# Softmax probabilities kept packed and multiplied with the values as 64-row tiles, in a gated cross-attention block on Trainium2

## The chip, the cores and the metric

The kernel runs on one core of a Trainium2 chip. The metric is the device time of one execution in microseconds; before the change it is 1895.37 us, the median of 3 runs (1894.49 to 1895.81).

## The reference

Everything is 32-bit float. There are 32 batches of 64 rows of width 512, 32 heads of width 128, 64 queries and 64 keys per batch and head. What is computed:

```python
x = x + tanh(g_xattn[0]) * xattn(layernorm(x), ctx, mask, bias, Wq, Wk, Wv, Wo)
x = x + tanh(g_ffn[0]) * ffn(layernorm(x), weight, bias, lora_A, lora_B, lora_start_indices)

def xattn(hq, hkv, mask, bias, Wq, Wk, Wv, Wo):
    q, k, v = (hq @ Wq), (hkv @ Wk), (hkv @ Wv)          # each reshaped to batch, 64, 32 heads, 128
    score = einsum('bqhd,bkhd->bhqk', q, k) / sqrt(128) + bias
    probs = softmax(where(mask, score, -inf))            # and 0 where masked
    return einsum('bhqk,bkhd->bqhd', probs, v).reshape(b, 64, 4096) @ Wo
```

`ffn` is a 512 by 512 layer with a bias and a low-rank addend per batch.

## The kernel before

**Precision.** Each operand of a product is split in two fp32r tiles, hi and lo (lo is what the rounding of hi left over). `mm3` (L172 to L176) makes a product of three matmuls (hi by hi, lo by hi, hi by lo). `both` (L192 to L197) makes it of two: the two parts of the left operand are loaded as weights in turn (L196 the hi part, L197 the lo part), and the hi and lo parts of the right one stream past side by side, so that a matmul is 256 columns wide. In the profile a matmul's operands stand as output<-moving,weights.

**Tiling.** The batches go in two halves of 16. A half is 1024 rows: two blocks of 512 columns (8 batches each), a block 4 tiles of 128 rows, and a tile holds two batches. The heads go in 16 groups of 2. A *slot* is one head on one block: 64 slots in a half, 128 in all. In slot s, TensorE's order is written out by hand (`slot` in the TensorE block): `queries_keys` (24 matmuls of 512 columns, to q_bank and k_bank), then half of `values` (even slots, 24 matmuls of 256 columns) or of `output` (odd slots, 12 matmuls of 512 columns), then `probabilities` of the slot before, the other half of `values` or `output`, `scores` of this slot, and `attention` of the slot before. The other engines have the same list of slots, each in its own order, and everything is bound by semaphores.

**Around the change.** `scores` (L326) multiplies, for each of a block's four tiles, the 128 queries by the 128 keys of the tile, 8 matmuls in a slot. Only the two 64 by 64 squares on the diagonal (a batch's own queries and keys) are used: VectorE scales them and adds bias and mask (L645, from `s_two`), so from there on the work is packed, 4 tiles of 64 keys in 256 columns: row maximum (L650), subtraction on GpSimd (L886), exp on ScalarE, row sum, and the division, on GpSimd (L897). The division writes the two squares of each tile into a 128 by 128 matrix `prob` whose other two squares stay zero from a memset at the start (L764). `probabilities` on TensorE (L319) turns the four matrices by four transposes into `t_bank` (512 columns of PSUM), ScalarE rounds them into the hi part of `pt`, VectorE makes the lo part (L600), and `attention` (L334) multiplies them with the values: 4 tiles, two weight loads of 128 by 128 (v_hi, v_lo), 256 moving columns each, 8 matmuls. ScalarE copies the lo half of the result (L483), VectorE adds the hi half (L654), and ScalarE and GpSimd split the sum for the next block's `output`. The columns of the context (`ctxt`) lie in the order of the batches.

Of the kernel before, what the change touches and what calls it, by code (L numbers as in the profile page):

```python
# [7 lines left out]
F32 = mybir.dt.float32  # L8
F32R = mybir.dt.float32r
I32 = mybir.dt.int32  # L10
U8 = mybir.dt.uint8
ALU = mybir.AluOpType
ACT = mybir.ActivationFunctionType
X = mybir.AxisListType.X

P = 128
NB = 32
S = 64
D = 512
H = 32  # L20
DH = 128
NL = 3
R = 16
C = D // P
HALVES = 2
T = NB * S // HALVES
TILES = T // P
BLK = 512
BLOCKS = T // BLK
PB = BLK // P  # L30
# [11 lines left out]
def flamingo_block(nc, x, ctxt, pair_bias, mask, wq, wk, wv, wo, g_xattn, g_ffn, wf, fbias, lora_a, lora_b,  # L42
# [16 lines left out]
    with ExitStack() as ctx:  # L59
        def sb(name, shape, dt=F32):  # L60
            return ctx.enter_context(nc.sbuf_tensor(name, shape, dt))
# [4 lines left out]
        def sem(name):  # L66
# [10 lines left out]
        o_w = [sb(f"wo_{p}", [P, HG, D], F32R) for p in ("hi", "lo")]  # L77

        qt = [sb(f"qt_{p}", [P, BLK], F32R) for p in ("hi", "lo")]
        kt = sb("kt", [P, PB, 2, P], F32R)  # L80
        v = [[sb(f"v{b}_{p}", [P, PB, HG * DH], F32R) for p in ("hi", "lo")] for b in range(2)]
        ot = [sb(f"ot_{p}", [P, HG, BLK], F32R) for p in ("hi", "lo")]
        pt = sb("pt", [P, PB, 2, P], F32R)
        raw_bias = [sb(f"raw_bias{b}", [P, HG, PB, S]) for b in range(BLOCKS)]
        bias_m = [sb(f"bias_m{b}", [P, PB, S]) for b in range(2)]
        score = sb("score", [P, PB, S])
# [1 line left out]
        score_b = sb("score_b", [P, PB, S])  # L88
        attn = sb("attn", [P, BLK])
        expd = sb("expd", [P, PB, S])  # L90
        prob = sb("prob", [P, PB, P])
        row_max = sb("row_max", [P, PB])
        row_sum = sb("row_sum", [P, PB])
        row_inv = sb("row_inv", [P, PB])
        row_scale = sb("row_scale", [P, PB])
# [19 lines left out]
        ident = sb("ident", [P, P])  # L115
# [14 lines left out]
        q_bank, k_bank = pb("q_bank"), pb("k_bank")  # L130
        vo_bank = [pb(f"vo_bank{i}") for i in range(2)]

        s_two = ctx.enter_context(nc.psum_tensor("s_two", [P, PB, 2, P], F32))
        pv_two = ctx.enter_context(nc.psum_tensor("pv_two", [P, PB, 2, P], F32))
        s_half, pv_half = ([two[:, 2 * i:2 * i + 2, :, :].rearrange("p a b c -> p (a b c)") for i in range(2)]
                           for two in (s_two, pv_two))
        t_bank = pv_half[0]

        xt_bank = [[pv_half, vo_bank], [[q_bank, k_bank], pv_half]]
        y_bank = [q_bank, k_bank]  # L140
# [14 lines left out]
        q_hi, k_hi, v_hi, pt_hi, ot_b, ot_hi, xt_hi, stage_hi, lora_hi, wq_hi, wk_hi, wv_hi, wo_hi = (  # L155
            sem(f"{m}_hi") for m in ("q", "k", "v", "pt", "ot_b", "ot", "xt", "stage", "lora", "wq", "wk", "wv", "wo"))
# [21 lines left out]
        def parts(pair, *at):  # L178
            return [p[at] for p in pair]

        def cols(i, n):
            return slice(i * n, (i + 1) * n)

        def by(bank, n):

            return bank[:, :].rearrange("p (a b) -> p a b", a=n)
# [6 lines left out]
        def both(pe, to, left, right):  # L193


            pe.matmul(to, left[0], right, start=True, stop=False)  # L196
            return pe.matmul(to, left[1], right, start=False, stop=True)  # L197

        def f32(part):

            return part.bitcast(F32)
# [74 lines left out]
        def _(pe):  # L276
# [41 lines left out]
            def probabilities(n):  # L318

                pe.wait_ge(prob_done, n)  # L320
                wait(pe, ot_sum, n - 1)
                for p in range(PB):
                    mm = pe.transpose(t_bank[:, cols(p, P)], prob[:, p, :], ident[:, :])  # L323
                mm.then_inc(t_ps, 1)

            def scores(n):  # L326
                pe.wait_ge(q_lo, n + 1)
                pe.wait_ge(k_lo, n + 1)
                wait(pe, score_done, n)
                for p in range(PB):  # L330
                    mm = both(pe, s_two[:, p, :, :], parts(qt, slice(None), cols(p, P)), kt[:, p, :, :])
                mm.then_inc(s_ps, 1)

            def attention(gg, s):  # L334

                n, vb, vh = STAGES * gg + s, v[(s - 1) // 2 % 2], (s - 1) % HG
                pe.wait_ge(v_lo, 2 * (BLOCKS * gg + (s - 1) // 2) + 2)
                pe.wait_ge(pt_lo, n)
                for p in range(PB):
                    mm = both(pe, pv_two[:, p, :, :], parts(vb, slice(None), p, cols(vh, DH)), pt[:, p, :, :])  # L340
                mm.then_inc(pv_ps, 1)

            def slot(gg, s, output_before=True, before_scores=NOTHING):
# [92 lines left out]
        def _(act):  # L436
            def hi(to, src, done, func=ACT.Copy, **kw):
                act.activation(to, src, func, **kw).then_inc(done, 1)  # L438
# [22 lines left out]
            def queries_keys(n):  # L461
                wait(act, s_ps, n)
                act.wait_ge(q_ps, n + 1)
                hi(qt[0][:, :], q_bank[:, :], q_hi)
                act.wait_ge(k_ps, n + 1)
                hi(kt[:, :, 0, :], by(k_bank, PB), k_hi)

            def values(gg, s, u):
                t, tb = BLOCKS * gg + s // 2, s // 2 % BLOCKS
# [4 lines left out]
            def probabilities(n):  # L474
                wait(act, pv_ps, n - 1)
                act.wait_ge(t_ps, n)
                hi(pt[:, :, 0, :], by(t_bank, PB), pt_hi)

            def attention(gg, s):
                n = STAGES * gg + s  # L480
                wait(act, ot_lo, n - 1)
                act.wait_ge(pv_ps, n)
                act.activation(by(attn, PB), pv_two[:, :, 1, :], ACT.Copy).then_inc(ot_b, 1)  # L483
                wait(act, o_ps, PB * (BLOCKS * gg + (s - 1) // 2))
                act.wait_ge(ot_sum, n)
                hi(ot[0][:, (s - 1) % HG, :], attn[:, :], ot_hi)
# [56 lines left out]
            load(starts_i[:, :], lora_starts.to_broadcast([P, NL + 1]), starts_in)  # L543
            load(lconst[:, :], lora_const, const_in)
            load(fb[:, :], fbias.to_broadcast([P, D]), fb_in)
            act.wait_ge(zero_done, 3)
            load(raw_a[:, :, 0:NL * R], lora_a, lora_a_in)
            load(raw_b[0:NL * R, :], lora_b, lora_b_in)
            pieces(0, range(C))
# [48 lines left out]
        def _(dve):  # L598
            def lo(to, src, of, done):
                dve.tensor_tensor(to, src, f32(of), ALU.subtract).then_inc(done, 1)  # L600
# [5 lines left out]
            def queries_keys(n):  # L606
                dve.wait_ge(q_hi, n + 1)
                lo(qt[1][:, :], q_bank[:, :], qt[0][:, :], q_lo)
                dve.wait_ge(k_hi, n + 1)
                lo(kt[:, :, 1, :], by(k_bank, PB), kt[:, :, 0, :], k_lo)  # L610

            def weights_o(grp):
                for u in range(HG):
# [17 lines left out]

            def probabilities(n):
                dve.wait_ge(pt_hi, n)
                lo(pt[:, :, 1, :], by(t_bank, PB), pt[:, :, 0, :], pt_lo)

            def scores(n, s):
                dve.wait_ge(bias_done, n + 1)
# [13 lines left out]

            def attention(n):
                dve.wait_ge(ot_b, n)
                dve.tensor_tensor(by(attn, PB), pv_two[:, :, 0, :], by(attn, PB), ALU.add).then_inc(ot_sum, 1)  # L654

            def row_scales(n, tb):
                dve.wait_ge(exp_done, n + 1)
# [103 lines left out]
                lo_scaled(b_w[1][:, :], raw_b[:, :], gate[:, 1:2], b_w[0][:, :], ab_lo)  # L761

            dve.memset(minus_half[:, :], -0.5).then_inc(half_done, 1)
            dve.memset(prob[:, :, :], 0.0).then_inc(zero_done, 1)  # L764
            dve.memset(raw_a[:, :, :], 0.0).then_inc(zero_done, 1)
            dve.memset(raw_b[:, :], 0.0).then_inc(zero_done, 1)
            pieces(0, range(C))
# [71 lines left out]
        def _(pool):  # L839
            def lo(to, src, of, done):  # L840
                pool.tensor_tensor(to, src, f32(of), ALU.subtract).then_inc(done, 1)  # L841
# [27 lines left out]
            def slot(gg, s, first=False, next_weights=True, before_shift=NOTHING, before_probabilities=NOTHING):  # L869
                n, grp, tb = STAGES * gg + s, gg + s // STAGES, s // 2 % BLOCKS  # L870

                wait(pool, prob_done, n)
                pool.wait_ge(bias_in[tb], 16 * (grp + 1))
                wait(pool, score_done, n - 1)
                pool.tensor_tensor(bias_m[s % 2][:, :, :], raw_bias[tb][:, s % HG, :, :],
                                   mask_add[:, cols(tb, PB), :], ALU.add).then_inc(bias_done, 1)
                if s % STAGES == 0:
                    weights_qk(grp, 1)
                if s % STAGES == 2 and next_weights:
                    weights_qk(grp + 1, 0)  # L880
                if s % STAGES == 3 and next_weights:
                    weights_v(grp + 1)
                before_shift()
                wait(pool, exp_done, n)
                pool.wait_ge(max_done, n + 1)
                pool.tensor_tensor(shifted[:, :, :], score[:, :, :],  # L886
                                   row_max[:, :].unsqueeze(2).to_broadcast([P, PB, S]),
                                   ALU.subtract).then_inc(shift_done, 1)
                before_probabilities()
                if not first:  # L890
                    attention_lo(n, s)
                    pool.wait_ge(ot_lo, n)
                wait(pool, t_ps, n)
                pool.wait_ge(rscale_done, n + 1)
                for b in range(2):
                    rows = cols(b, S)
                    last = pool.tensor_tensor(prob[rows, :, rows], expd[rows, :, :],  # L897
                                              row_scale[rows, :].unsqueeze(2).to_broadcast([S, PB, S]), ALU.mult)
                last.then_inc(prob_done, 1)

            def add_bias(half, tiles):
                for i in tiles:
# [7 lines left out]
            weights_v(0)  # L910
            deviations(0, 0, 0)
            weights_qk(0, 0)
            pool.wait_ge(zero_done, 1)
            for half in range(HALVES):
                first = G * half
                pool.wait_ge(mask_in, 16 * (half + 1))
# [74 lines left out]
```

## Time and profile before

| | |
|---|---|
| median of 3 runs | 1895.37 us |
| profiled execution, first to last instruction (span) | 1893.1 us |
| what lies around the span, median less span | 2.3 us |
| TensorE busy, matmuls / weight loads | 96% / 85% of the span |
| VectorE, GpSimd, ScalarE busy | 62%, 42%, 35% |
| mean granted TensorE clock | 0.986 of full speed |

For the profiled execution the profile gives its span alone, so its own time is not listed; the sum is made against the span. A row of a timeline is: start, length, engine, line, operation, output<-inputs, partitions and columns, and in brackets the engine's idle time before it and what ended it. PE is TensorE's matmuls, PEld its weight loads, DVE VectorE, ACT ScalarE, POOL GpSimd. Matmuls are pipelined, so that their lengths overlap: what one costs is read from start to start.

### The profile page before, as it was taken

Reading aid. Unit: us, or ns where it says so; the run is one execution under the profiler, and the core shown is the slowest. Engines: PE = TensorE matmul, PEld = TensorE weight load, DVE = VectorE, ACT = ScalarE, POOL = GpSimd, SP = SyncE. Lnnn points to the kernel's source line nnn. Section 1 sums busy time; section 2 is a strip of 40 time slices with the busy share of each in tenths; the row PEclk is TensorE's granted clock in tenths of the full one; section 3 lists DMA queues with packets and bytes.
Section 4 is the critical chain, followed back from the end, with each engine's and each line's share of the span. In section 5 each row is a group of like instructions: output and inputs, shape, how many; then the busy total and the mean of one; then the engine's idle time right before and its main releaser. Section 6 shows DMA issues by size and latency. Waiting matters only on the chain.

```text
span 1893.1 us, 30362 instructions
## 1 busy us (share of the span) xinstructions
PE 1826.3 (96%) x10656; PEld 1615.6 (85%) x10656; DVE 1174.6 (62%) x2178; ACT 659.6 (35%) x1216; POOL 790.2 (42%) x872
## 2 busy tenths in 40 slices
PE   4899999999999999999879999999999999999988
PEld 4788888888888888888669888888888888888876
DVE  4866666666666666666756666666666666666674
ACT  3333333333333333333223333333333333333331
POOL 2343434444444444444324434344444444444423
PEclk9999999999999999999889999999999999999999
DMA  4211111111111111101231011111111011111001
GB/s 156 79 56 50 44 55 55 50 36 41 55 50 54 46 55 50 48 30 56 67 111 69 29 50 55 50 44 55 55 50 42 36 55 50 55 44 55 17 1 45
DMA packets 37343, 99.60 MB, mean 53 GB/s; under 512 B 5136, under 2 KB 5392, under 8 KB 37312
## 3 DMA queue, kind: packets, MB, share of 16 engines
q1 hardware_dynamic: 35136, 96.09, 15.1%
q10 hardware_dynamic: 2176, 3.10, 0.5%
q8 instruction: 19, 0.31, 0.1%
q14 instruction: 12, 0.10, 0.0%
HBM read 94.98 MB, written 4.19 MB: 52 GB/s over the span
## 4 chain that ended last, share of the span: by engine, by line
PE 94%; DVE 4%; ACT 1%; issue 1%; ACTq 1%; POOL 0%; DVEq 0%; POOLq 0%
PE vo_bank L174 13%; PE vo_bank L176 13%; PE vo_bank L175 13%; PE q_bank L174 7%; PE q_bank L175 7%; PE q_bank L176 7%; PE k_bank L174 6%; PE k_bank L176 6%; PE k_bank L175 6%; PE s_two L196 3%; PE s_two L197 3%; PE pv_two L196 3%; PE pv_two L197 3%; PE pv_two L323 3%; ACTq L533 1%
## 5 line engine op out<-in xcount | busy, mean ns | idle before, releaser
L886 POOL TENSOR_TENSOR shifted<-score,row_max 128x256 f32<-128x256 f32 x128 | 78.5, 613 | 795.7 <-DVE row_max L650 795.7
L174 PE MATMUL vo_bank<-wv_hi,ct_hi 128*128 128x256 f32 x1024 | 295.4, 289 | 18.9 <-POOL wv_lo L841 18.9
L176 PE MATMUL vo_bank<-wv_hi,ct_lo 128*128 128x256 f32 x1024 | 290.7, 284 | 0.0
L175 PE MATMUL vo_bank<-wv_lo,ct_hi 128*128 128x256 f32 x1024 | 290.5, 284 | 0.0
L629 DVE TENSOR_TENSOR acc<-vo_bank,acc 128x512 f32<-128x512 f32 x256 | 176.9, 692 | 93.6 <-PE vo_bank L176 90.4
L174 PEld LDWEIGHTS vo_bank<-wv_hi,ct_hi 128*128 128x128 f32 x1024 | 197.0, 192 | 21.3 <-issue 18.9
L841 POOL TENSOR_TENSOR ot_lo<-attn,ot_hi 128x512 fp32r<-128x512 f32 x128 | 165.3, 1291 | 118.4 <-ACT ot_hi L438 118.4
L174 PE MATMUL vo_bank<-wo_hi,ot_hi 128*128 128x512 f32 x512 | 207.2, 405 | 7.2 <-DVE acc L629 5.5
L174 PE MATMUL q_bank<-xt_hi,wq_hi 128*128 128x512 f32 x512 | 203.0, 396 | 2.8 <-DVE xt_lo L600 2.8
L175 PE MATMUL q_bank<-xt_lo,wq_hi 128*128 128x512 f32 x512 | 202.0, 394 | 0.0
L176 PE MATMUL vo_bank<-wo_hi,ot_lo 128*128 128x512 f32 x512 | 201.6, 394 | 0.0
L175 PE MATMUL vo_bank<-wo_lo,ot_hi 128*128 128x512 f32 x512 | 201.0, 393 | 0.0
L176 PE MATMUL q_bank<-xt_hi,wq_lo 128*128 128x512 f32 x512 | 200.4, 391 | 0.0
L174 PE MATMUL k_bank<-ct_hi,wk_hi 128*128 128x512 f32 x512 | 199.2, 389 | 0.0
L175 PE MATMUL k_bank<-ct_lo,wk_hi 128*128 128x512 f32 x512 | 199.2, 389 | 0.0
L176 PE MATMUL k_bank<-ct_hi,wk_lo 128*128 128x512 f32 x512 | 199.2, 389 | 0.0
L175 PEld LDWEIGHTS vo_bank<-wv_lo,ct_hi 128*128 128x128 f32 x1024 | 197.0, 192 | 2.5
L483 ACT ACTIVATE attn<-pv_two 128x512 f32<-128x512 f32 x128 | 76.7, 599 | 345.2 <-PE pv_two L197 345.1
L176 PEld LDWEIGHTS vo_bank<-wv_hi,ct_lo 128*128 128x128 f32 x1024 | 196.7, 192 | 0.0
L600 DVE TENSOR_TENSOR v_lo<-vo_bank,v_hi 128x512 fp32r<-128x512 f32 x128 | 88.1, 688 | 162.9 <-ACT v_hi L438 162.9
L600 DVE TENSOR_TENSOR kt<-k_bank,kt 128x512 fp32r<-128x512 f32 x128 | 88.5, 692 | 150.0 <-ACT kt L438 150.0
L897 POOL TENSOR_TENSOR prob<-expd,row_scale 64x256 f32<-64x256 f32 x256 | 157.5, 615 | 31.4 <-DVE row_scale L663 23.8
(128 smaller groups left out, 4011.3 us busy)
## 6 DMA issues: line engine op xcount, KB each, us to landing
raw_q<-in_wq SPq DMA_DIRECT2D x31, 512.0 KB, 3.3
raw_k<-in_wk SPq DMA_DIRECT2D x31, 512.0 KB, 4.9
raw_v<-in_wv SPq DMA_DIRECT2D x31, 512.0 KB, 5.7
raw_bias<-in_pair_bias SPq DMA_DIRECT2D x62, 256.0 KB, 2.6
raw_o<-in_wo SPq DMA_DIRECT2D x31, 512.0 KB, 3.2
stage<-in_ctxt SPq DMA_DIRECT2D x16, 256.0 KB, 4.4
acc<-in_x SPq DMA_DIRECT2D x16, 256.0 KB, 4.2
out<-y_out SPq DMA_DIRECT2D x16, 256.0 KB, 2.0
```

Source lines behind the costliest of these rows:

```text
L174: pe.matmul(to, left[0], right[0], start=first, stop=False)
L175: pe.matmul(to, left[0], right[1], start=False, stop=False)
L176: return pe.matmul(to, left[1], right[0], start=False, stop=last)
L196: pe.matmul(to, left[0], right, start=True, stop=False)
L197: return pe.matmul(to, left[1], right, start=False, stop=True)
L323: mm = pe.transpose(t_bank[:, cols(p, P)], prob[:, p, :], ident[:, :])
L483: act.activation(by(attn, PB), pv_two[:, :, 1, :], ACT.Copy).then_inc(ot_b, 1)
L600: dve.tensor_tensor(to, src, f32(of), ALU.subtract).then_inc(done, 1)
L629: dve.tensor_tensor(acc[:, tile, :], vo_bank[p % 2][:, :], acc[:, tile, :], ALU.add).then_inc(acc_done, 1)
L841: pool.tensor_tensor(to, src, f32(of), ALU.subtract).then_inc(done, 1)
L886: pool.tensor_tensor(shifted[:, :, :], score[:, :, :], row_max[:, :].unsqueeze(2).to_broadcast([P, PB, S]), ALU.subtract).then_inc(shift_d ...
L897: last = pool.tensor_tensor(prob[rows, :, rows], expd[rows, :, :], row_scale[rows, :].unsqueeze(2).to_broadcast([S, PB, S]), ALU.mult)
```

## The change

`prob` stays packed: 128 rows (two batches of 64 queries) by 4 tiles by 64 keys. Two transposes of 128 by 128, each over two tiles, turn it: rows 0 to 63 of `pt` then hold keys of the first tile of a pair, rows 64 to 127 those of the second. `attention` takes 64 rows at a time: for each of four t, for the hi and the lo part of v, the upper and the lower half of the rows in turn, 16 matmuls of 128 moving columns with weights of 64 by 128. The two halves write to different PSUM banks. GpSimd's division is one instruction over 128 rows in place of two over 64. The hi and lo steps of `pt` are over 256 columns, not 512. So that keys and values fall in the order which this needs, the host permutes the context's columns (of four batches in two tiles, the middle two change places), the scores' right side is read from `kt` in 64-column runs that undo the permutation, and the two steps that add up the result write into `attn` in the old order. The memset of `prob` and the waits for it go.

```diff
-        kt = sb("kt", [P, PB, 2, P], F32R)
+        kt = sb("kt", [P, 2, 2, 2, 2, S], F32R)
-        pt = sb("pt", [P, PB, 2, P], F32R)
+        pt = sb("pt", [P, 2, PB, S], F32R)
-        prob = sb("prob", [P, PB, P])
+        prob = sb("prob", [P, PB, S])
-        pv_two = ctx.enter_context(nc.psum_tensor("pv_two", [P, PB, 2, P], F32))
+        pv_two = ctx.enter_context(nc.psum_tensor("pv_two", [P, 2, 2, PB, S], F32))
-        t_bank = pv_half[0]
+        t_bank = pv_half[0][:, 0:2 * P]
+        def pair_rows(bank):
+            return bank[:, :].rearrange("p (j r m) -> p r j m", j=2, r=2)
+        def half_sum(part):
+            return pv_two[:, :, part, :, :].rearrange("p r (j a) s -> p r j (a s)", j=2)
+        def score_right(p):
+            return kt[:, :, p // 2, :, p % 2, :]
...
-                for p in range(PB):
-                    mm = pe.transpose(t_bank[:, cols(p, P)], prob[:, p, :], ident[:, :])
+                for j in range(2):
+                    mm = pe.transpose(t_bank[:, cols(j, P)], prob[:, cols(j, 2), :].rearrange("p a b -> p (a b)"),
+                                      ident[:, :])
...
-                    mm = both(pe, s_two[:, p, :, :], parts(qt, slice(None), cols(p, P)), kt[:, p, :, :])
+                    mm = both(pe, s_two[:, p, :, :], parts(qt, slice(None), cols(p, P)), score_right(p))
...
-                for p in range(PB):
-                    mm = both(pe, pv_two[:, p, :, :], parts(vb, slice(None), p, cols(vh, DH)), pt[:, p, :, :])
+                for t in range(PB):
+                    for part in range(2):
+                        for r in range(2):
+                            rows = cols(r, S)
+                            mm = pe.matmul(pv_two[:, r, :, t, :], vb[part][rows, t, cols(vh, DH)], pt[rows, :, t, :],
+                                           start=part == 0, stop=part == 1)
...
-                hi(pt[:, :, 0, :], by(t_bank, PB), pt_hi)
+                hi(pt[:, 0, :, :].rearrange("p t s -> p (t s)"), t_bank, pt_hi)
...
-                act.activation(by(attn, PB), pv_two[:, :, 1, :], ACT.Copy).then_inc(ot_b, 1)
+                act.activation(pair_rows(attn), half_sum(1), ACT.Copy).then_inc(ot_b, 1)
...
-                lo(pt[:, :, 1, :], by(t_bank, PB), pt[:, :, 0, :], pt_lo)
+                thi, tlo = (pt[:, part, :, :].rearrange("p t s -> p (t s)") for part in range(2))
+                lo(tlo, t_bank, thi, pt_lo)
...
-                dve.tensor_tensor(by(attn, PB), pv_two[:, :, 0, :], by(attn, PB), ALU.add).then_inc(ot_sum, 1)
+                dve.tensor_tensor(pair_rows(attn), half_sum(0), pair_rows(attn), ALU.add).then_inc(ot_sum, 1)
...
-            dve.memset(prob[:, :, :], 0.0).then_inc(zero_done, 1)
...
-                for b in range(2):
-                    rows = cols(b, S)
-                    last = pool.tensor_tensor(prob[rows, :, rows], expd[rows, :, :],
-                                              row_scale[rows, :].unsqueeze(2).to_broadcast([S, PB, S]), ALU.mult)
-                last.then_inc(prob_done, 1)
+                pool.tensor_tensor(prob[:, :, :], expd[:, :, :],
+                                   row_scale[:, :].unsqueeze(2).to_broadcast([P, PB, S]), ALU.mult).then_inc(prob_done, 1)
...
+    ctxt = a["ctx_4096"].reshape(HALVES, BLOCKS, 2, 2, 2, S, C, P)
-        "ctxt": a["ctx_4096"].reshape(HALVES, BLOCKS, BLK, C, P).transpose(0, 1, 3, 4, 2).reshape(-1, P, BLK),
+        "ctxt": ctxt.transpose(0, 1, 6, 7, 2, 4, 3, 5).reshape(-1, P, BLK),
```

## Rows read from the trace of the kernel before

**Rows 1.** The page: engines' busy time, and the chain that ended last by engine.

```profile
PE 1826.3 (96%) x10656; PEld 1615.6 (85%) x10656; DVE 1174.6 (62%) x2178; ACT 659.6 (35%) x1216; POOL 790.2 (42%) x872
...
PE 94%; DVE 4%; ACT 1%; issue 1%; ACTq 1%; POOL 0%; DVEq 0%; POOLq 0%
```

**Rows 2.** Waits, all engines: us in total, times, longest.

```profile
PE vo_bank L174 <- POOL wv_lo L841: 18.9, 1, 18.9
...
PE pv_two L323 <- POOL prob L897: 8.0, 4, 2.9
```

**Rows 3.** Busy time by stretch: two steady slots, then one at a half's end.

```profile
480.00:507.00 27.00, 27.00 (x164) 24.06 (x163) 17.95 (x32) 9.95 (x19) 10.73 (x12) 1.00 0.13 42
908.00:911.00 3.00, 3.00 (x15) 2.77 (x14) 2.47 (x4) 2.55 (x5) 0.00 (x0) 0.50 0.00 0
```

**Rows 4.** Timeline of TensorE's matmuls in steady slots.

```profile
507.58 0.28 PE L196 MATMUL pv_two<-pt,v_hi 128*128 128x256 f32 x1
507.70 0.28 PE L197 MATMUL pv_two<-pt,v_lo 128*128 128x256 f32 x1
...
508.54 0.40 PE L174 MATMUL q_bank<-xt_hi,wq_hi 128*128 128x512 f32 x1
508.77 0.40 PE L175 MATMUL q_bank<-xt_lo,wq_hi 128*128 128x512 f32 x1
...
516.74 0.60 PE L323 MATMUL pv_two<-ident,prob 128*128 128x128 f32 x4
517.09 0.48 PE L174 MATMUL vo_bank<-wo_hi,ot_hi 128*128 128x512 f32 x1
517.40 0.40 PE L175 MATMUL vo_bank<-wo_lo,ot_hi 128*128 128x512 f32 x1
...
521.86 0.40 PE L174 MATMUL q_bank<-xt_hi,wq_hi 128*128 128x512 f32 x1
```

**Rows 5.** TensorE's groups with shapes apart: count, busy us and mean ns.

```profile
L174 PE MATMUL vo_bank<-wv_hi,ct_hi 128*128 128x256 f32 x1024 | 295.4, 289 | 18.9 <-POOL wv_lo L841 18.9
...
L196 PE MATMUL pv_two<-pt,v_hi 128*128 128x256 f32 x512 | 130.0, 286 | 1.4 <-DVE pt L600 1.4
...
L323 PE MATMUL pv_two<-ident,prob 128*128 128x128 f32 x512 | 77.9, 275 | 8.0 <-POOL prob L897 8.0
```

**Rows 6.** Timeline of matmuls and weight loads after an idle time.

```profile
914.78 0.19 PEld L174 LDWEIGHTS vo_bank<-wo_hi,ot_hi 128*128 128x128 f32 x1 [1.16 <-POOL ot_lo L841]
914.78 0.50 PE L174 MATMUL vo_bank<-wo_hi,ot_hi 128*128 128x512 f32 x1 [0.72 <-POOL ot_lo L841]
914.89 0.19 PEld L175 LDWEIGHTS vo_bank<-wo_lo,ot_hi 128*128 128x128 f32 x1
915.11 0.40 PE L175 MATMUL vo_bank<-wo_lo,ot_hi 128*128 128x512 f32 x1
```

**Rows 7.** The same, where the clock is halved.

```profile
907.33 1.06 PE L367 MATMUL q_bank<-ident,xn 128*128 128x128 f32 x4
...
908.18 1.06 PE L367 MATMUL k_bank<-ident,xn 128*128 128x128 f32 x4
...
909.67 0.41 PE L196 MATMUL pv_two<-pt,v_hi 128*128 128x256 f32 x1
...
909.88 0.41 PE L197 MATMUL pv_two<-pt,v_lo 128*128 128x256 f32 x1
```

**Rows 8.** Timeline of the other engines in an odd slot.

```profile
513.26 1.28 POOL L897 TENSOR_TENSOR prob<-expd,row_scale 64x256 f32<-64x256 f32 x2 [0.19 <-DVE row_scale L663]
...
517.43 0.60 ACT L438 ACTIVATE pt<-pv_two 128x512 fp32r<-128x512 f32 x1 [1.58 <-PE pv_two L323]
518.06 0.69 DVE L600 TENSOR_TENSOR pt<-pv_two,pt 128x512 fp32r<-128x512 f32 x1 [0.43 <-ACT pt L438]
```

**Rows 9.** Groups of the other engines at 256 columns.

```profile
L886 POOL TENSOR_TENSOR shifted<-score,row_max 128x256 f32<-128x256 f32 x128 | 78.5, 613 | 795.7 <-DVE row_max L650 795.7
...
L438 ACT ACTIVATE expd<-shifted 128x256 f32<-128x256 f32 x128 | 51.6, 403 | 4.0 <-POOL shifted L886 4.0
```

**Rows 10.** Timeline of all engines at the end of the second half.

```profile
1837.88 1.28 POOL L897 TENSOR_TENSOR prob<-expd,row_scale 64x256 f32<-64x256 f32 x2 [0.19 <-DVE row_scale L663]
...
1839.21 1.11 PE L323 MATMUL pv_two<-ident,prob 128*128 128x128 f32 x4 [1.09 <-POOL prob L897]
1839.40 0.99 DVE L703 TENSOR_SCALAR xn<-acc,mean_var,rstd 128x512 f32<-128x512 f32 x2
1840.12 1.06 PE L367 MATMUL q_bank<-ident,xn 128*128 128x128 f32 x4
```

More of the change, by code:

```diff
@@ L133, in flamingo_block @@
         s_two = ctx.enter_context(nc.psum_tensor("s_two", [P, PB, 2, P], F32))
-        pv_two = ctx.enter_context(nc.psum_tensor("pv_two", [P, PB, 2, P], F32))
-        s_half, pv_half = ([two[:, 2 * i:2 * i + 2, :, :].rearrange("p a b c -> p (a b c)") for i in range(2)]
-                           for two in (s_two, pv_two))
-        t_bank = pv_half[0]
+        pv_two = ctx.enter_context(nc.psum_tensor("pv_two", [P, 2, 2, PB, S], F32))
+        s_half = [s_two[:, 2 * i:2 * i + 2, :, :].rearrange("p a b c -> p (a b c)") for i in range(2)]
+        pv_half = [pv_two[:, i, :, :, :].rearrange("p a b c -> p (a b c)") for i in range(2)]
+        t_bank = pv_half[0][:, 0:2 * P]
[5 more added lines that the diff above has]
+            return kt[:, :, p // 2, :, p % 2, :]
         xt_bank = [[pv_half, vo_bank], [[q_bank, k_bank], pv_half]]
@@ L465, in queries_keys @@
                 act.wait_ge(k_ps, n + 1)
-                hi(kt[:, :, 0, :], by(k_bank, PB), k_hi)
+                hi(kt[:, 0, :, :, :, :].rearrange("p j a r s -> p (j a r s)"), k_bank[:, :], k_hi)
             def values(gg, s, u):
@@ L545, in _ @@
             load(fb[:, :], fbias.to_broadcast([P, D]), fb_in)
-            act.wait_ge(zero_done, 3)
+            act.wait_ge(zero_done, 2)
             load(raw_a[:, :, 0:NL * R], lora_a, lora_a_in)
@@ L609, in queries_keys @@
                 dve.wait_ge(k_hi, n + 1)
-                lo(kt[:, :, 1, :], by(k_bank, PB), kt[:, :, 0, :], k_lo)
+                khi, klo = (kt[:, part, :, :, :, :].rearrange("p j a r s -> p (j a r s)") for part in range(2))
+                lo(klo, k_bank[:, :], khi, k_lo)
             def weights_o(grp):
@@ L912, in _ @@
             weights_qk(0, 0)
-            pool.wait_ge(zero_done, 1)
             for half in range(HALVES):
```

## The prediction, on record before the changed kernel ran

> **What bounds the kernel now.** I read the page first. TensorE is busy for 96% of the span, and the chain that ended last lies on it for 94% [rows 1]. A busy share says little where matmuls overlap, so the waits come next: TensorE's largest is 18.9 us, once, at the start, and the next to bear on this change is 8.0 us in 4 waits for `prob` [rows 2]. In 128 slots that is nothing per slot. The busy time by stretch confirms it: in 27 us of steady slots TensorE is busy for all 27.00 at full clock, VectorE for 17.95, ScalarE for 9.95 and GpSimd for 10.73 [rows 3]. So a steady slot costs what TensorE's list of matmuls costs, and every step on another engine has slack.
>
> The timeline gives the prices at full clock. A slot with `output` is 521.86 - 508.54 = 13.32 us. Attention is its 8 matmuls from 507.58 to 508.54, 0.96 us or 0.120 each; a 512-column matmul costs 0.23 [rows 4]. So 256 more columns cost 0.107, and a matmul has some 0.013 beside its columns. Four transposes last 0.60, the last one some 0.275 of it [rows 4, 5]: (0.60 - 0.275) / 3 = 0.108 from start to start, though only 128 columns pass, whose stream by the slope above is 0.053. What takes the rest is seen after an idle time: the second weight load starts 0.11 after the first, with the first matmul's stream [rows 6]. A load of 128 columns thus occupies the loading path for about 0.107, and a transpose costs its load. At the halved clock a transpose costs (908.18 - 907.33) / 4 = 0.21 and a 256-column matmul 0.21 [rows 3, 7], twice as much, as a load counted in the array's clock must. Today 256 columns just cover a load. After the change 128 don't. That is the whole question.
>
> **The change, part by part.**
>
> *Transposes.* Two of four go: 2 x 0.108 = 0.216 us a slot, x 128 slots = 27.7 us, all on TensorE's own list, so on the path. Nothing can hide this gain while TensorE never waits.
>
> *Attention.* Before: 8 loads, 8 x 256 columns, 0.96 us. After: 16 loads of 64 rows by 128 columns and 16 matmuls of 128 columns, in turn on two halves of the rows. No row here shows a 64-row tile, so both ends come from other rows. If the halves run beside each other and a 64-row load is no bound either, a pair costs its stream and the fixed part, 0.053 + 0.013 = 0.066, and attention 8 x 0.066 = 0.53 us: 0.43 saved, 55 us in all. If nothing overlaps, each matmul costs its load, 16 x 0.108 = 1.73 us: 0.77 more, 98.6 us; at today's 0.120 each, 1.92 us and 123 us more. I take the case between. The two halves have their own rows, operands and PSUM banks, so loads as well as streams of a pair lie beside each other, but within one half the next load still takes 0.108 as in the transposes, the nearest row by shape: 8 x 0.108 = 0.87 us. The first load of the next slot's q product now hides behind 128 columns (0.053), where it had 256 (0.107): 0.05 of it shows. So 0.92 us, 0.04 saved, 5.6 us in all.
>
> The Trainium skill bears on the overlap ("TensorE: Matmul & The Clock Gate", Part 3: Packing small matmuls): matmuls of different row groups run concurrently, started some 4 ns apart, and a load overlaps matmuls in flight where its row group differs. It also says (Part 2) that a load's time follows its columns, not its rows. By both, attention would be near 8 loads long, which is my middle case; no run here shows a tile of fewer rows.
>
> *Scores.* The same 8 matmuls; their right side is now read in four runs of 64 columns in place of two of 128. Matmuls that read one run of 256 (289 ns mean) and two of 128 (286 ns) are recorded alike [rows 5], so I take four at nothing. Were each 0.01 dearer, it would be 10 us in all; a gain has no ground.
>
> *Side engines.* `prob` takes one instruction over 128 rows; the same 256 columns over 128 rows in the subtraction take 613 ns against 2 x 0.64 [rows 8, 9], 0.67 us earlier. ScalarE's hi step falls from 0.60 to about 0.40, which exp takes for 256 columns [rows 8, 9]; VectorE's lo step falls from 0.69, to some 0.4 at half its columns. In a steady slot all of it is slack: `prob` was done at 514.54 and the transposes began at 516.74 [rows 4, 8]. It counts where TensorE waits, at the four waits of rows 2. But at a half's end the next transposes wait for `xn` at once [rows 10], so most of the 0.67 is given back; I take nothing, with 4 x 0.67 = 2.7 us as the bound on the gain. The steps that write `attn` keep their 512 columns and are covered by slack of microseconds; cover gone, 0.1 each would be 26 us, but nobody on TensorE's list waits for them in a steady slot. The memset of `prob` at the start lies before TensorE's first matmul, which waits for weights [rows 2]: nothing. Host permutation: same bytes, same DMAs. No wait is added.
>
> Sum: -27.7 - 5.6 = -33.3 us. The span 1893.1 becomes 1859.8; with the 2.3 us between it and the median, **1862 us**.
>
> **Rivals.**
>
> *Loads one after the other (slower).* If the loading path takes one load at a time whatever rows it goes to, attention is load-bound at 16 x 0.108 = 1.73 us. The first two rows of an idle start [rows 6] show two loads 0.11 apart, but of the same rows, so they fit both. Price: +98.6 - 27.7 = +71 us, 1966 us (1990 at 0.120 each). It decides from the point where 16 loads take more than 0.96 + 0.216 = 1.18 us, 0.074 each: if even a third of each load isn't hidden by its partner, the gain is gone. For it: a load is the costly part of the transposes too. Against it: separate halves of the array. Chance 0.20.
>
> *The array empties at each change of tile height (slower).* A steady matmul is recorded 0.28 long and costs 0.12, so 0.16 of its way lies under the next ones [rows 4]. If going from 128 rows to 64 and back waits for the array to run empty, each of 256 changes shows 0.16, or 0.27 with the next load in the open: 42 to 69 us, less 33: 1904 to 1931. Nothing in the trace changes height, so nothing speaks for or against. Chance 0.12. The Trainium skill has it as a rule ("TensorEngine Tiling (Array Packing)", Key Properties): changing the tiling mode drains TensorE. Wholly true here, it would turn my gain into this rival; no run here shows it yet.
>
> *Loads overlap, streams do not.* 16 x 0.066 = 1.06 us, +0.10 us a slot, 13 us: 1895.4 - 27.7 + 13 = 1881. Chance 0.12.
>
> *Everything overlaps, short loads.* -27.7 - 55: 1813. Chance 0.06.
>
> *The change doesn't pay what it says.* Partial costs cancel the transposes and it stays within 4 us of 1895. Chance 0.04.
>
> **How the numbers follow.** The forecast has 0.46; its own range, from pairs at 0.100 (-41.6 us) to pairs at 0.120 (-21.6 us), is 1854 to 1874. About 0.2% (3.8 us) is what a measurement of this kernel can tell from no change. Faster by more: 0.46 + 0.12 + 0.06 = 0.64. Within: 0.04. Slower: 0.20 + 0.12 = 0.32. The forecast, the streams in turn and the emptied array hold 0.74 with the cancelled case, so the range must reach to the serial loads: 1848 (the forecast's 1854 less the bounds that I took at nothing) to 1968.
>
> **What would show it.** Right: the transposes are 256 in all, two in a slot, from start to start still 0.108; attention's 16 matmuls start in pairs, a pair every 0.11, 0.9 us in a slot; the slot with `output` falls from 13.32 to about 13.06 us; TensorE still has no waits in steady slots. Serial loads would show as loads 0.107 apart without gaps and attention at 1.7 us. An emptied array would show as a gap of 0.16 or more before attention's first matmul and before q_bank's first. Wrong altogether: a new wait of TensorE for `pt` or `prob`, or scores slower than 0.120 each.

## The result, and the profile after

| | before | after |
|---|---|---|
| median of 15 runs each | 1895.3 us | 1898.26 us |
| ratio, 95% interval | | 1.0018, 1.001 to 1.0025 |
| span of the profiled execution | 1893.1 us | 1896.4 us |
| transposes of `prob` | 512 | 256 |
| attention's matmuls | 1024 of 128 rows, 256 columns | 2048 of 64 rows, 128 columns |

The forecast was 33 us faster; the kernel became 3 us slower. That is 0.16%, less than the 0.2% that the prediction takes as the least a measurement can tell from no change, but with 15 runs on each side the interval excludes a ratio of 1. The changed kernel's page, engines' busy time and the chain by engine, to lay beside [rows 1]:

```profile
PE 1834.0 (97%) x11424; PEld 1598.3 (84%) x11424; DVE 1139.5 (60%) x2177; ACT 631.8 (33%) x1216; POOL 713.2 (38%) x744
...
PE 94%; DVE 4%; issue 1%; ACT 1%; ACTq 1%; POOL 0%; DVEq 0%
```

GpSimd, VectorE and ScalarE lost 77, 35 and 28 us of work, and none of it shows in the time, as TensorE's list still sets it. The same stretch as [rows 3], engines in the same order:

```profile
480.00:507.00 27.00, 27.00 (x175) 23.67 (x174) 17.07 (x32) 9.38 (x18) 9.52 (x10) 1.00 0.15 48
```

No new wait stands in the steady slots: none of TensorE's waits occurs more than 4 times in the 128 slots. The one for `prob`, in [rows 2] 8.0 us, is shorter:

```profile
PE vo_bank L184 <- POOL wv_lo L857: 19.2, 1, 19.2
...
PE pv_two L333 <- POOL prob L911: 4.5, 4, 1.9
```

So the expected gain must have gone inside TensorE's list. The timeline of its matmuls, for an odd slot as in [rows 4] (line numbers have moved: L333 are the transposes, L354 is attention, L184 the first matmul of a product):

```profile
509.53 0.50 PE L184 MATMUL q_bank<-xt_hi,wq_hi 128*128 128x512 f32 x1
509.87 0.39 PE L185 MATMUL q_bank<-xt_lo,wq_hi 128*128 128x512 f32 x1
...
512.36 0.39 PE L184 MATMUL k_bank<-ct_hi,wk_hi 128*128 128x512 f32 x1
...
517.80 0.38 PE L333 MATMUL pv_two<-ident,prob 128*128 128x128 f32 x2
517.94 0.48 PE L184 MATMUL vo_bank<-wo_hi,ot_hi 128*128 128x512 f32 x1
518.25 0.40 PE L185 MATMUL vo_bank<-wo_lo,ot_hi 128*128 128x512 f32 x1
...
521.50 0.28 PE L206 MATMUL s_two<-kt,qt_hi 128*128 128x256 f32 x1
521.62 0.28 PE L207 MATMUL s_two<-kt,qt_lo 128*128 128x256 f32 x1
521.84 0.33 PE L354 MATMUL pv_two<-pt,v_hi 64*128 64x128 f32 x2
522.00 0.28 PE L354 MATMUL pv_two<-pt,v_lo 64*128 64x128 f32 x2
522.11 0.27 PE L354 MATMUL pv_two<-pt,v_hi 64*128 64x128 f32 x2
...
522.67 0.28 PE L354 MATMUL pv_two<-pt,v_lo 64*128 64x128 f32 x2
522.87 0.50 PE L184 MATMUL q_bank<-xt_hi,wq_hi 128*128 128x512 f32 x1
523.21 0.39 PE L185 MATMUL q_bank<-xt_lo,wq_hi 128*128 128x512 f32 x1
```

Three things are to be seen. From the first transpose to the second matmul of `output` behind them it takes 518.25 - 517.80 = 0.45 us, where [rows 4] have 517.40 - 516.74 = 0.66: the 0.21 of the two transposes has come. Attention's matmuls run in pairs (x2; all but the first are recorded 0.28 long as one alone is, so both start together), a pair every 0.11 us: that part has come as well. But both ends of attention have a seam, a place where one kind of matmul follows another and the step is longer. From the last matmul of scores to the first pair it takes 0.22 in place of 0.12, the first pair takes 0.16 in place of the 0.11 of the others, from the last pair to q_bank's first matmul it is 0.20, and that one holds the next back for 0.34 in place of 0.23. The slot as a whole takes 522.87 - 509.53 = 13.34 us, and took 13.32.

The weight loads at the same place say what a seam is made of:

```profile
521.39 0.19 PEld L206 LDWEIGHTS s_two<-kt,qt_hi 128*128 128x128 f32 x1
521.51 0.19 PEld L207 LDWEIGHTS s_two<-kt,qt_lo 128*128 128x128 f32 x1
521.83 0.19 PEld L354 LDWEIGHTS pv_two<-pt,v_hi 64*128 64x128 f32 x2
521.94 0.19 PEld L354 LDWEIGHTS pv_two<-pt,v_lo 64*128 64x128 f32 x2
...
522.61 0.19 PEld L354 LDWEIGHTS pv_two<-pt,v_lo 64*128 64x128 f32 x2
522.87 0.19 PEld L184 LDWEIGHTS q_bank<-xt_hi,wq_hi 128*128 128x128 f32 x1
522.98 0.19 PEld L185 LDWEIGHTS q_bank<-xt_lo,wq_hi 128*128 128x128 f32 x1
```

Within scores the next load starts when the matmul before it starts (521.51, beside the matmul of 521.50), and within attention a load starts some 0.05 behind the pair before it. At a change of height it starts later. The last matmul of scores starts at 521.62, and its 256 columns pass until about 521.73 (an estimate, from the 0.107 of the prediction); the load for 64-row tiles starts only at 521.83, and the next load 0.11 behind it, with no earlier columns beside it. On the way back the last pair starts at 522.67, its 128 columns are through at about 522.72 by the same estimate, and the load starts at 522.87.

### The profile page after: what moved, and what is told of

Same layout as the page of the kernel before. It is cut to its first block, busy times and chain, and to the rows that moved or that the text cites. A ratio compares the mean times of both kernels' runs of the same rounds, so it can differ in the third digit from the quotient of the medians.

```text
span 1896.4 us, 31768 instructions
## 1 busy us (share of the span) xinstructions
PE 1834.0 (97%) x11424; PEld 1598.3 (84%) x11424; DVE 1139.5 (60%) x2177; ACT 631.8 (33%) x1216; POOL 713.2 (38%) x744
## 4 chain that ended last, share of the span: by engine, by line
PE 94%; DVE 4%; issue 1%; ACT 1%; ACTq 1%; POOL 0%; DVEq 0%
PE vo_bank L184 13%; PE vo_bank L186 13%; PE vo_bank L185 13%; PE q_bank L184 8%; PE pv_two L354 7%; PE q_bank L185 7%; PE q_bank L186 7%; PE k_bank L184 6%; PE k_bank L186 6%; PE k_bank L185 6%; PE s_two L206 3%; PE s_two L207 3%; PE pv_two L333 1%; ACTq L548 1%; DVE stats L710 1%
## 5 line engine op out<-in xcount | busy, mean ns | idle before, releaser
L184 PE MATMUL vo_bank<-wv_hi,ct_hi 128*128 128x256 f32 x1024 | 295.8, 289 | 19.2 <-POOL wv_lo L857 19.2
L184 PE MATMUL q_bank<-xt_hi,wq_hi 128*128 128x512 f32 x512 | 215.4, 421 | 3.1 <-DVE xt_lo L615 3.1
L184 PEld LDWEIGHTS vo_bank<-wv_hi,ct_hi 128*128 128x128 f32 x1024 | 197.2, 193 | 21.6 <-issue 19.1
L184 PE MATMUL vo_bank<-wo_hi,ot_hi 128*128 128x512 f32 x512 | 207.1, 404 | 4.2 <-DVE acc L645 4.2
L184 PE MATMUL k_bank<-ct_hi,wk_hi 128*128 128x512 f32 x512 | 199.2, 389 | 0.0
L453 ACT ACTIVATE kt<-k_bank 128x512 fp32r<-128x512 f32 x128 | 76.6, 599 | 259.4 <-PE k_bank L186 259.4
```

What stands on the lines that cost most here:

```text
L184: pe.matmul(to, left[0], right[0], start=first, stop=False)
```

## The experiments

Theory H says that each change between 128-row and 64-row tiles costs time by itself. The rivals put the loss on short matmuls at their seams (S), or on attention's new layout (D, P). Each time below is a median of 4 to 6 runs, one case excepted; the kernel before was measured again beside them, at 1895.16 us for four of the runs and 1895.18 us for the two with one matmul more and the one without lo by lo.

**Attention at full height.** In the changed kernel:

```diff
-                        for r in range(2):
-                            rows = cols(r, S)
-                            mm = pe.matmul(pv_two[:, r, :, t, :], vb[part][rows, t, cols(vh, DH)], pt[rows, :, t, :],
-                                           start=part == 0, stop=part == 1)
+                        mm = pe.matmul(pv_two[:, t % 2, :, t, :], vb[part][:, t, cols(vh, DH)], pt[:, :, t, :],
+                                       start=part == 0, stop=part == 1)
```

> The changed kernel, but attention uses all 128 rows: 8 matmuls of 128 columns in place of 16 of 64 rows (each product sums the two tiles' batches, so that part of the computation is changed). Theory H (each change between 128-row and 64-row tiles costs TensorE about 0.17 us, two per slot, 256 in all): the 8 loads take 8 x 0.108 = 0.87 us and no change of height is left, so 1895.3 - 27.7 (two transposes fewer) - 5.6 = 1862 us, between 1857 and 1868. Rival S (short matmuls lose at their seams, since 128 columns do not cover the next load, whatever the height): the loss stays, 1885 to 1900 us.

Measured: 1860.36 us, ratio to before 0.9815 (0.9799 to 0.9832). (What it computes isn't attention any more, as each product mixes two batches; the order of the work is the same.) This is the sum of the forecast, without changes of height. Its timeline, from the last matmul of scores on:

```profile
510.99 0.28 PE L207 MATMUL s_two<-kt,qt_lo 128*128 128x256 f32 x1
511.11 0.22 PE L352 MATMUL pv_two<-pt,v_hi 128*128 128x128 f32 x1
511.17 0.28 PE L352 MATMUL pv_two<-pt,v_lo 128*128 128x128 f32 x1
511.28 0.27 PE L352 MATMUL pv_two<-pt,v_hi 128*128 128x128 f32 x1
...
511.84 0.28 PE L352 MATMUL pv_two<-pt,v_lo 128*128 128x128 f32 x1
511.95 0.44 PE L184 MATMUL q_bank<-xt_hi,wq_hi 128*128 128x512 f32 x1
512.23 0.40 PE L185 MATMUL q_bank<-xt_lo,wq_hi 128*128 128x512 f32 x1
...
514.77 0.39 PE L184 MATMUL k_bank<-ct_hi,wk_hi 128*128 128x512 f32 x1
```

There is no gap on the way in: the first matmul comes after the usual 0.12, the second already 0.06 behind it, the others every 0.11. On the way out it is 0.28 in place of 0.23: the 0.05 of a load that 128 columns don't cover. From the last matmul of scores to the second of q_bank it takes 1.24 us, in the changed kernel 523.21 - 521.62 = 1.59. Rival S is out: short matmuls of full height have almost no seam. The difference to the changed kernel, 1898.26 - 1860.36 = 37.9 us, is 0.30 us for each of 128 slots, for two changes of height. Laid side by side, the timelines put 0.20 of the 0.35 on the way in (from the last matmul of scores to attention's second step, 522.00 - 521.62 = 0.38 against 511.17 - 510.99 = 0.18) and 0.15 on the way out (from attention's last step to q_bank's second matmul, 0.54 against 0.39). The difference of 0.05 comes back in the q product: from its second matmul to the first of `k_bank` it takes 512.36 - 509.87 = 2.49 in the changed kernel and 514.77 - 512.23 = 2.54 here. No run shows why.

**Four changes of height.** In the changed kernel, attention cut in two around the scores:

```diff
-            def attention(gg, s):
+            def attention(gg, s, ts=range(PB)):
...
-                for t in range(PB):
+                for t in ts:
...
-                scores(STAGES * gg + s)
-                attention(gg, s)
+                attention(gg, s, range(2))
+                scores(STAGES * gg + s)
+                attention(gg, s, range(2, PB))
```

> The changed kernel with attention cut in two: tiles 0 and 1 before the scores, 2 and 3 behind them. Same instructions, four changes of height per slot in place of two. Theory H: two more at 0.17 us in 128 slots, +44 us, 1942 us, between 1930 and 1955. Rival S: only one more seam each way behind short matmuls, at most 0.05 us each as the load of 0.107 exceeds a stream of 0.053: +6 to +13 us, 1904 to 1911. Rival D (the loss is a one-time price of attention's data, not of the change of height): 1898 +- 3.

Measured: 1945.65 us, ratio to before 1.0267 (1.025 to 1.0284). Against the changed kernel that is 47.4 us more, 0.37 us a slot for two more changes, with the same instructions. D would have it at nothing, S at 13 us at most. A part of the step from 0.30 to 0.37 shows in this run's timeline: of the 0.05 that came back in the q product little is left, 511.13 - 508.60 = 2.53 us from its second matmul to the first of `k_bank`, where the changed kernel has 2.49. The price belongs to each visit to the other height, not to each matmul in it.

**The halves one after the other.** In the changed kernel, the loop over r outermost in attention:

```diff
-                for t in range(PB):
-                    for part in range(2):
-                        for r in range(2):
-                            rows = cols(r, S)
+                for r in range(2):
+                    rows = cols(r, S)
+                    for t in range(PB):
+                        for part in range(2):
```

> The changed kernel with the 8 matmuls of the upper half first and the 8 of the lower half behind them, not in turn. If the pairs overlap because the halves alternate in the order of instructions: each load now waits for the one before it in its own half, 16 x 0.107 = 1.71 us in place of 0.89, +0.82 x 128 = +105 us, about 2003 us. If the halves overlap in whatever order they are issued: 1898 us.

Measured: 1959.93 us, in a single run, 62 us above the changed kernel: between the two expectations, and neither is right. The timeline of one slot's attention shows why:

```profile
523.83 0.27 PE L354 MATMUL pv_two<-pt,v_lo 64*128 64x128 f32 x1
523.94 0.33 PE L354 MATMUL pv_two<-pt,v_hi 64*128 64x128 f32 x2
524.05 0.33 PE L354 MATMUL pv_two<-pt,v_lo 64*128 64x128 f32 x2
524.16 0.33 PE L354 MATMUL pv_two<-pt,v_hi 64*128 64x128 f32 x2
524.27 0.33 PE L354 MATMUL pv_two<-pt,v_lo 64*128 64x128 f32 x2
524.44 0.27 PE L354 MATMUL pv_two<-pt,v_hi 64*128 64x128 f32 x1
```

Four matmuls run alone, then four times two, then four alone: 12 steps of 0.11, not 16 and not 8. Within a half v_hi and v_lo alternate, so two v_hi side by side are of different halves (the second of two starts up to 0.06 behind the first): the lower half's first matmul runs beside the upper half's fifth, ahead of three that were issued before it. At 0.11 a step, four steps more are 0.45 us, x 128 = 57 us of the 62. Issuing the halves in turn is thus worth these 62 us. That TensorE reaches just so far ahead in its list is read from this one run.

**One matmul more, of full height or of half.** In the kernel before, between scores and attention, into columns that attention overwrites (`rows` is `slice(None)` in the first run, `cols(0, S)` in the second):

```diff
                 pe.wait_ge(pt_lo, n)
...
+                pe.matmul(pv_two[:, 0, 0, :], vb[0][rows, 0, cols(vh, DH)], pt[rows, 0, 0, :], start=True, stop=True)
                 for p in range(PB):
```

> The kernel before with one more matmul per slot between scores and attention, 128 rows and 128 columns, whose result attention overwrites. Control for the next run. It costs its weight load: 0.11 x 128 = +14 us, 1909 us, by every theory.

> The same extra matmul with 64 rows in place of 128, in a kernel where nothing else is a 64-row tile. Theory H (the price belongs to the change of height, 0.37 us for the way there and back as in the cut-in-two run): 0.11 + 0.37 = 0.48 us per slot, +61 us, 1957 us, between 1945 and 1965. Rival P (the loss belongs to attention's new layout: its banks, its interleaved writes, its pairs): a single 64-row matmul costs what the 128-row one costs, 1909 us.

Measured: 1909.69 us with the full one (ratio 1.0081, 1.0066 to 1.0096), 1948.12 us with the half one (1.0282, 1.0266 to 1.0298). The full one costs 14.5 us, its load. The half one, which has half the data, costs 52.9 us: 38.4 us or 0.30 us a slot more, in a kernel whose layout, banks and attention are untouched. Rival P is out. The expectation had taken the 0.37 of the run with four changes; what repeats is the 0.30 of the full-height run. Matmuls and loads around the half one:

```profile
521.11 0.28 PE L197 MATMUL s_two<-kt,qt_lo 128*128 128x256 f32 x1
521.32 0.18 PEld L340 LDWEIGHTS pv_two<-pt,v_hi 64*128 64x128 f32 x1
521.32 0.32 PE L340 MATMUL pv_two<-pt,v_hi 64*128 64x128 f32 x1
521.57 0.19 PEld L196 LDWEIGHTS pv_two<-pt,v_hi 128*128 128x128 f32 x1
521.57 0.39 PE L196 MATMUL pv_two<-pt,v_hi 128*128 128x256 f32 x1
521.80 0.28 PE L197 MATMUL pv_two<-pt,v_lo 128*128 128x256 f32 x1
```

Both its load and the load after it start late, as in the changed kernel: 0.21 after the last matmul's start and 0.25 after its own.

**Two transposes, no 64-row tile.** From the changed kernel: its context order, packed `prob` and two transposes stay, but ScalarE and VectorE write the transposed squares as block diagonals into a `pt` of the old size, whose zeros are set once at the start; attention is 8 matmuls of 128 rows and 256 columns again, and its output is placed so that `attn` comes out in order.

```diff
-        pt = sb("pt", [P, 2, PB, S], F32R)
+        pt = sb("pt", [P, PB, 2, 2, S], F32R)
...
-        pv_two = ctx.enter_context(nc.psum_tensor("pv_two", [P, 2, 2, PB, S], F32))
+        pv_two = ctx.enter_context(nc.psum_tensor("pv_two", [P, 2, 2, 2, 2, S], F32))
...
+        def square(part, x):
+            rows = cols(x, S)
+            return t_bank[rows, :].rearrange("p (t s) -> p t s", t=PB), pt[rows, :, part, x, :]
...
+                        mm = pe.matmul(pv_two[:, t // 2, :, :, t % 2, :], vb[part][:, t, cols(vh, DH)],
+                                       pt[:, t, :, :, :].rearrange("p a b s -> p (a b s)"),
+                                       start=part == 0, stop=part == 1)
...
-                hi(pt[:, 0, :, :].rearrange("p t s -> p (t s)"), t_bank, pt_hi)
+                for x in range(2):
+                    src, to = square(0, x)
+                    last = act.activation(to, src, ACT.Copy)
+                last.then_inc(pt_hi, 1)
...
```

> Two transposes per slot as in the changed kernel, but the transposed probabilities are written as block diagonals (zeros beside them, set once at the start) and multiplied as before, 128 rows and 256 columns, 8 matmuls. ScalarE and VectorE each write pt in two steps over 64 rows. Theory H: nothing changes height, only the two transposes are missing: 1895.3 - 27.7 = 1867.6 us, between 1864 and 1871. Rival S gives the same, since no short matmul is left. Rival W: the two-step writes (about 0.2 us more on ScalarE, 0.15 on VectorE per slot) make TensorE wait for pt: above 1872 us, with a wait of TensorE for pt in the steady slots.

Measured: 1867.58 us, ratio to before 0.9855 (0.9839 to 0.9872). The two transposes are worth 27.6 us, as the prediction's first term has it. TensorE waits for `pt` once (L357 is attention here), as before the change, so rival W is out:

```profile
PE pv_two L357 <- DVE pt L660: 1.5, 1, 1.5
```

**The same without lo by lo.** The block-diagonal version, in scores and attention, with the product of the two lo parts left out:

```diff
-                    mm = both(pe, s_two[:, p, :, :], parts(qt, slice(None), cols(p, P)), score_right(p))
+                    pe.matmul(s_two[:, p, :, :], qt[0][:, cols(p, P)], score_right(p), start=True, stop=False)
+                    mm = pe.matmul(s_two[:, p, 0, :], qt[1][:, cols(p, P)], kt[:, 0, p // 2, :, p % 2, :],
+                                   start=False, stop=True)
...
-                        mm = pe.matmul(pv_two[:, t // 2, :, :, t % 2, :], vb[part][:, t, cols(vh, DH)],
-                                       pt[:, t, :, :, :].rearrange("p a b s -> p (a b s)"),
-                                       start=part == 0, stop=part == 1)
+                    pe.matmul(pv_two[:, t // 2, :, :, t % 2, :], vb[0][:, t, cols(vh, DH)],
+                              pt[:, t, :, :, :].rearrange("p a b s -> p (a b s)"), start=True, stop=False)
+                    mm = pe.matmul(pv_two[:, t // 2, 0, :, t % 2, :], vb[1][:, t, cols(vh, DH)],
+                                   pt[:, t, 0, :, :].rearrange("p b s -> p (b s)"), start=False, stop=True)
```

> The block-diagonal version without the products of two lo parts in scores and attention: 8 of its 16 matmuls there pass 128 columns in place of 256 (the smallest of the four products is left out, as it is in every other matmul of the kernel). Theory L (a 128-column matmul of 128 rows costs its load, 0.11, so little less than the 0.120 of 256 columns): 8 x 0.01 x 128 = 10 us less, some of it given back where the next slot's load is less covered, 1858 to 1864 us. Rival C (columns are what costs): 8 x 0.053 x 128 = 54 us less, 1813 us.

Measured: 1862.03 us, ratio to before 0.9828 (0.9816 to 0.9841), 5.6 us less than the version it comes from. A quarter of the columns of scores and attention is gone and nearly no time: the loads set it, as theory L has it.

## Why the prediction was wrong

The first statement held: TensorE's own list bounds the steady slots, and everything taken off the other engines is worth nothing.

*Transposes*, -27.7 us: right. The block-diagonal run, which has this term alone, gives -27.6.

*Attention*, -5.6 us: right in its own terms (its slope of 0.107 for 256 columns is 0.23 - 0.120 = 0.11 by the rows it shows, which moves the term by less than 1 us). Pairs of 64-row tiles overlap, loads and matmuls both, at one pair in 0.11 us, and an uncovered load shows 0.05 at the end. The full-height run, which has both terms and no 64-row tile, gives 1895.16 - 1860.36 = 34.8 us for the 33.3 of the sum.

*Scores and side engines*, nothing: right. Scores still start every 0.12 us.

*The change of tile height*, left out of the sum: this is the step that failed. The prediction had it as a rival at 0.12, priced 0.16 to 0.27 us for each of 256 changes, and left it out of the forecast, which got 0.46, with no row against it. What the runs show in its place is 0.30 us for two changes (full height against changed: 37.9 us; half against full extra matmul: 38.4 us) and 0.37 where attention is cut in two. -34.8 + 37.9 is the +3 us that was measured.

The rival was the mechanism. Its lower price was nearly the right size, 256 x 0.16 = 41 us (the prediction has 42) against the 37.9 measured; its upper price, with the whole next load in the open each time, was too high at 69. With the lower price the kernel would have come out 8 us slower. It came out 3 us slower, 3 of the 5 us between because the changes cost 37.9, and 1.5 because the rest of the sum was worth 34.8 and not 33.3.

Beside it the prediction quoted a rule of the Trainium skill ("TensorEngine Tiling (Array Packing)", Key Properties): changing the tiling mode drains TensorE. The traces agree with it as far as they go: the load behind the change begins about 0.10 us after the last columns of scores and 0.15 after those of the last pair, and not beside them. What I lacked was not the mechanism but a reason to give it so little; the rows held none against it, and the one rule that spoke to it spoke for it. A rule with nothing against it should have been in the forecast. With the rival at its lower price, the forecast would have been 1862 + 41 = 1903 us.

That the changes of height add up to about the gain, so that the kernel's time hardly moved and lies inside the stated range, is chance. In the block-diagonal run, with no 64-row tile, the kernel is 28 us faster, with two visits in a slot it is 50 us slower.

*Serial loads*, the rival at 0.20, is out: pairs start together. The two rivals in which streams take turns or loads don't bind are out too, by the 0.11 from pair to pair.

Three things stay open. The timelines divide the price into the way in and the way out, but no run has one without the other, and none shows whether it depends on what the array does at the time. Nor is it shown that the array is wholly empty when the late load starts: the last matmul of scores is recorded until 521.62 + 0.28 = 521.90, the load behind it starts at 521.83, and recorded ends are modelled. A load that isn't taken ahead across a change of height would look the same. And no run puts two slots' attention in one visit; by the price above, an estimate, that would save about half of the 37.9 us.

## What to carry to other kernels

Half-height tiles can pay only where the work done at that height in one visit saves more than the way there and back: here a round trip of 0.30 us stood against attention steps of 0.11 in place of 0.12, some 0.05 us a slot ((1867.58 - 1860.36) / 128). If packing is wanted for another reason (here fewer transposes), keep the height of the neighbours and pay with zeros: here columns that passed under a weight load were nearly free, 5.6 us for a quarter of the columns of scores and attention, so that a block diagonal in 256 columns cost nearly the same as 128 packed ones. Where loads bind, count loads, not columns.

## What the runs showed of the hardware that I had not expected

Matmuls of different row halves did not keep the order in which they were issued: with eight of the upper half ahead of eight of the lower, the first lower one started ahead of three upper ones. And a single 64 by 128 matmul among taller ones, the smallest there, cost 0.41 us (52.9 us / 128), against 0.11 for twice the rows (14.5 us / 128) and 0.23 for a matmul of 512 columns.
